# Decoder layer on one Trainium2 core: another distribution of the key and value projections over the batches of a selective scan

## What is computed

```
x = x + mamba(layernorm(x))           # selective scan, 1024 channels, 16 states each
x = x + cross_attention(ctx_1024, keys and values from layernorm(x))   # in the reference's order of arguments (v, k, q)
x = x + ffn(layernorm(x))             # weights binarised, 512 -> 2048 -> 512

# of the scan, per batch element:
xz = rmsnorm(u) @ W_in ;  x, z = split(xz)
x  = silu(conv(x) + b) ;  x_dbl = x @ W_x
dt = softplus(x_dbl[:, :64] @ W_dt + b_dt)
h  = exp(dt * A) * h + (dt * x) * B   # for each of 224 steps
y  = sum over the 16 states of h * C, + x * D
out = u + (y * silu(z)) @ W_out

# of the cross attention, per batch element, 750 context rows:
k = ctx @ Wk + bk ;  v = ctx @ Wv
```

## Time and profile before

| what | us |
|---|---|
| median of three runs | 3401.52 (3398.46 to 3403.88) |
| the profiled execution, its own time | 3404.25 |
| its span in the trace | 3402.7 |
| PE (TensorE matmul) busy | 3155.0 |
| DVE (VectorE) busy | 2577.2 |
| ACT (ScalarE) busy | 2261.3 |
| POOL (GpSimd) busy | 1737.7 |

### The profile page before, as it was taken

The page is one execution under the profiler, slowest core; times in us unless marked ns, Lnnn a source line. Parts: engine busy times, 40 slices in busy tenths (PEclk is TensorE's granted clock), DMA queues, the critical chain, the costliest instruction groups (busy, mean ns, idle before and its releaser), DMA issues. The chain is left out here.

```text
span 3402.7 us, 59176 instructions
## 1 busy us (share of the span) xinstructions
PE 3155.0 (93%) x20736; PEld 2196.4 (65%) x20736; DVE 2577.2 (76%) x4546; ACT 2261.3 (66%) x5049; POOL 1737.7 (51%) x1194
## 2 busy tenths in 40 slices
PE   6699989998999999999998899999999999899999
PEld 5566656665567566666665566666666666578887
DVE  4799999999999999999986577777777777523232
ACT  4678777777777777777764577777777777622222
POOL 2678788788887888778875000100000000055554
PEclk8799999999999999999999899999999999999999
DMA  6677677676767767677665121211211221210100
GB/s 176 178 191 190 180 184 176 174 197 176 185 177 188 187 167 186 184 186 186 171 173 166 54 73 55 89 49 48 85 59 48 73 71 61 63 61 25 48 27 25
DMA packets 286725, 424.98 MB, mean 125 GB/s; under 512 B 28801, under 2 KB 226177, under 8 KB 281954
## 3 DMA queue, kind: packets, MB, share of 16 engines
q1 hardware_dynamic: 278957, 412.62, 44.3%
q10 hardware_dynamic: 7477, 8.59, 0.9%
HBM read 320.12 MB, written 101.02 MB: 124 GB/s over the span
## 5 line engine op out<-in xcount | busy, mean ns | idle before, releaser
L808 POOL TENSOR_TENSOR a_hs<-a_rep,a_bmat 128x896 f32<-128x896 f32 x512 | 1061.1, 2095 | 336.4 <-PE a_yps L319 323.6
L442 ACT ACTIVATE a_states<-a_rep,a_a_neg 128x224 f32<-128x224 f32 x2048 | 795.6, 439 | 194.8 <-DVE a_hs L708 181.9
L701 DVE TENSOR_TENSOR_SCAN a_states<-a_states,a_hs 128x900 f32<-128x900 f32 x384 | 779.0, 2029 | 100.1 <-ACT a_states L442 99.5
L1433 DVE CUSTOM_DVE_ANT_0 b_sc<-sps,early_mask 112x375 f32<-112x375 f32 x1024 | 499.6, 544 | 135.4 <-PE sps L1179 129.5
L1320 ACT ACTIVATE b_sc<-b_sc,b_nmax 112x750 f32<-112x750 f32 x512 | 467.3, 913 | 0.7 <-DVE b_nmax L1439 0.7
L1193 PEld LDWEIGHTS b_tps<-ident,b_sc 112*125 112x125 f32 x3072 | 357.3, 189 | 169.8 <-issue 118.7
L341 PE MATMUL a_work<-early_scan_hT,w_in 128*128 128x224 f32 x2048 | 432.1, 370 | 16.7 <-issue 13.2
L341 PEld LDWEIGHTS a_work<-early_scan_hT,w_in 128*128 128x128 f32 x2048 | 411.7, 202 | 42.0 <-issue 30.2
L1193 PE MATMUL b_tps<-ident,b_sc 112*125 112x112 f32 x3072 | 404.8, 281 | 26.8 <-DVE b_pT L1447 18.2
L708 DVE TENSOR_TENSOR a_hs<-a_states,a_cmat 128x896 f32<-128x896 f32 x384 | 419.0, 1091 | 13.2
L1573 POOL TENSOR_SCALAR b_x_var<-mv 112x2 f32<-112x2 f32 x16 | 3.4, 214 | 814.2 <-DVE mv L1484 814.2
(11 more groups left out here) (193 smaller groups left out, 4735.3 us busy)
## 6 DMA issues: line engine op xcount, KB each, us to landing
a_rep<-du_scratch SPq DMA_DIRECT2D x512, 224.0 KB, 5.5
w_in<-W_in_dram SPq DMA_DIRECT2D x128, 512.0 KB, 4.5
du_scratch<-early_du SPq DMA_DIRECT2D x15, 1792.0 KB, 6.5
ctx<-ctxT_dram SPq DMA_DIRECT2D x48, 500.0 KB, 5.8
v_scratch<-kv_out SPq DMA_DIRECT2D x96, 250.0 KB
k_scratch<-kv_out SPq DMA_DIRECT2D x96, 250.0 KB, 4.3
b_keys<-k_scratch SPq DMA_DIRECT2D x8, 1500.0 KB, 9.2
b_v<-v_scratch SPq DMA_DIRECT2D x8, 1500.0 KB
```

What stands on the lines that cost most here:

```text
L442: e = act.activation(rows(states[:, g % DA, :])[:, q, 1:ROW], rep[tile % REPS][:, j, 0, :], ACT.Exp, scale=a_neg[:, g % SLOTS, q:q + 1])
L701: dve.tensor_tensor_scan(state if g % G4 else whole, state, whole, 0.0, ALU.mult, ALU.add).then_inc(S["scan"], 1)
L808: pool.tensor_tensor(hs[g % RING][:, :, 1:ROW], rep[tile % REPS][:, j, 1, :].unsqueeze(1).broadcast_to([P, Q, L]), bmat[b % 2][:], ALU.mul ...
L1433: dve.tensor_tensor_reduce(out=sc[buffer_of(block)][:, j, cols], in0=sps[0:TT, j, 0:HALF], in1=mask[:, block % 2, cols], scale=-1.0, scala ...
```

## The change

Only the three tuples change, that is, the slots in which units run.

```diff
         first = (16, 17, 22, 24, 25, 28, 29, 31, 33)
-        usual = (1, 3, 5, 12, 13, 18, 20, 21, 24, 25, 29)
-        last_but_one = (1, 2, 3, 4, 5, 12, 13, 17, 18, 19, 20, 21, 22, 23, 24, 25, 26, 28, 29, 30)
-        last = (-1, 1, 2, 3, 5, 6, 7, 12, 13, 14, 15, 16, 17, 18, 19, 20, 21, 22, 23, 24)
+        usual = (1, 3, 5, 6, 12, 13, 18, 20, 21, 24, 25, 29)
+        last_but_one = (1, 3, 5, 6, 12, 13, 18, 20, 21, 22, 24, 25, 28, 29)
+        last = (1, 3, 5, 6, 12, 14, 15, 17, 18, 20, 21, 22, 24)
         kv_slot = ([*first] + [w * SLOTS + BEHIND + at for w in range(1, B - 2) for at in usual]
                    + [(B - 2) * SLOTS + BEHIND + at for at in last_but_one] + [(B - 1) * SLOTS + BEHIND + at for at in last])
```

## The result

| what | before | after |
|---|---|---|
| median of the runs, us | 3401.52 (3398.4 to 3403.9) | 3415.69 (3413.4 to 3426.3) |
| ratio, 95% interval | | 1.0050 (1.0032 to 1.0068) |
| profiled execution, us | 3404.25 | 3420.86 |
| its span | 3402.7 | 3419.3 |
| batches 1 to 13 | 1434.4 | 1473.1 |

The changed kernel is slower, by 14 us in the medians and 16.6 in the profiled executions; 10 were predicted, within 3395 to 3427. The ratio goes by the means of the runs, the times here are medians. All of them are of undisturbed executions; one of the four of run 9 took 5987.64 us and is left out. By the last four rows it is +38.7 - 5.6 - 13.9 - 0.3 = 18.9 us from batch 1 to the end; what lies ahead of batch 1, where nothing changed, was 2.3 us shorter in this execution (batch 1 begins at 197.7 us, not 200.0).

What follows compares the result with a forecast made beforehand. Usual batches were taken as bound by TensorE and VectorE in turn, the last two by their units. +32.9 for the usual batches and -22.9 for the last two gave +10.0 us: 3411.5 us, range 3395 to 3427.

Steps and rivals of the forecast that it cites:

- the room at +16 and +17: TensorE's waits at slots 16 and 17 of a batch's scan: 6.2 + 6.4 = 12.6 us over 13 batches absorb added work.
- the 4.1 us at +8: TensorE's wait before the sum at slot 8: lies ahead of the added unit, so it can't use it.
- The 2.7 at +21: TensorE's wait before the dt products' second half, slot 21: takes up nothing, since lateness returns through ScalarE and the gap moves.
- Rival 1: Usual batches absorb the added unit, with the wait at +21 as room; only the 22.9 gain counts: 3379 us; chance 0.14.
- Usual batches: Batches 1 to 13: 13 added units of 3.5 us each, less 12.6 us of room, cost 32.9 us.
- rival 2: Longer slow clock stretches behind +21 in all 13 usual batches: 13.5 us more, +23.5 in all, 3425 us; chance 0.10.
- DVE's residual wait: VectorE's residual sums wait for the later out projections, about 1 us a batch, adding nothing to the 2.5 per batch.
- The last two batches: Batches 14 and 15 lose 13 units; VectorE's waits fall from 36.9 to 14.0 us, gaining 22.9.
- rival 3: Batches 14 and 15 go down to VectorE's own time: waits shrink to 5, 32 gained, 3402 us; chance 0.11.
- rival 4: Emptied TensorE runs slow in batches 14 and 15, out projections 3 us late in both: +20.5, 3422 us; chance 0.05.

Runs made afterwards that it cites:

- run 9: Kernel before, with a third store buffer in batches 14 and 15 and thirteen of their units shortened to one step of four; 3386.86 us, 0.9955 of before.
- run 1: Changed kernel, with the unit added to batches 1 to 13 at slot 6 (+6) instead of +10; 3405.2 us, 1.0007 of before.
- run 2: Kernel before, with the matmuls of the unit at +9 done twice into the same bank in batches 1 to 13; 3435.93 us, 1.0103 of before.
- run 3: Kernel before, with the matmuls of the unit at +7 done twice into the same bank in batches 1 to 13; 3423.99 us, 1.0063 of before.
- run 4: Kernel before, with thirteen units of batches 14 and 15 doing one of four steps, all copies and stores kept; 3400.84 us, 0.9995 of before.
- run 8: Kernel before, with a third buffer between ScalarE's copies and the stores in batches 14 and 15; 3393.3 us, 0.9972 of before.
- run 7: Changed kernel, with the added unit at +6 instead of +10 and the sum of +20 done twice in batches 1 to 13; 3366.77 us, 0.9893 of before.
- run 10: The kernel of run 7, with half of the matmuls of the unit at +9 done once more; 3354.63 us, 0.9861 of before.
- run 5: Kernel before, with TensorE doing the sum over states of +20 twice in batches 1 to 13; 3378.23 us, 0.9929 of before.

## Why the prediction was right, and where its sizes were off

**The sign and its cause: right.** The forecast was the case in which the added unit finds only the room at +16 and +17. Both went as written: nothing left at +16, 0.15 us at +17 in batch 3, and 10.8 us used, where 12.6 were allowed. That the 4.1 us at +8 can't be used from +10 is shown by run 1, which could use them. That the 2.7 at +21 takes up nothing is shown by its 35.0 us in the change and in runs 1 to 3. Rival 1 is refuted with it.

**Usual batches: +38.7 instead of +32.9.** Divided at the wait of +21, from the sum at +8 to the dt products batches 1 to 13 went from 553.9 to 588.1 us, +34.2; from there to the next +8 from 876.6 to 882.1, +5.5; the ends, ahead of the first +8 and behind the last, make -0.9. The first part is the term itself, 45.5 - 10.8 = 34.7, and stands 1.3 above the forecast. In it, too, the clock is seen: seven batches of the change in which it stays low for longer behind +8 take 45.7 to 46.0 us from +8 to the dt products, the other six 44.4 to 44.7. Before, both kinds took 42.0 to 42.8, because the wait at +16 took up the difference. The second part the forecast had at zero ("behind +21 everything is shifted and nothing changed"). It is rival 2 in part, 5.5 us of its 13.5: of the 13 batches four had a long slow stretch behind +21, and now eight have one. The rival had supposed all 13. That four more got one, and not nine or none, nothing in the prediction foresaw; in this term the forecast stayed near by luck. The Trainium skill, TensorE: Matmul & The Clock Gate, Part 1, says that the gate's steps don't start with the kernel, and batches of equal work that differ by 1.6 us (111.4 and 109.8 before) agree with it.

**DVE's residual wait: right, and costing nothing.** 15.9 us appeared at L723, 1.2 a batch. Run 2 paid as much as the change's usual batches without any such wait.

**The last two batches: -19.5 instead of -22.9, for a reason that was half wrong.** Batch 14 kept 7.8 us of waits instead of 5.4, batch 15 10.6 instead of 8.6. The stores were slow before the next phase's loads began, which the prediction had as the reason: in before, a store of keys landed after 3.6 us in the median of batches 1 to 13, after 6.0 between 1634 and 1800 us, where units stand closer together and none of those loads has been issued, and after 6.8 behind 1800. In the tail of batch 15 the wo issue took 8.30 us and not 5.79: the copy behind it waited 6.85 us, and the one at 1869.60 waited 6.68 for a store. The failed step is the statement that the units bind these batches up to +23 and the stores only behind it. Runs 4, 8 and 9 show what binds instead: relief of PE alone brings 4.3 us, of the stores alone 8.2, of both 15.6. By batch it is 0.6, 5.5 and 5.4 in batch 14, which the stores bound, and 3.7, 2.7 and 10.2 in batch 15, in which PE and stores bound in turn. The change takes away unit, copy and store together and brought 19.5. The size came out nearly right because it was bounded by DVE's waits, which are the same whoever is behind them; for the cause that the prediction named, it was luck.

**The sum.** +38.7 - 19.5 - 0.3 = +18.9 from batch 1 on, -2.3 for batch 0, +16.6 in the profiled executions; +14.2 in the medians. Two terms were off by 5.8 and 3.4 us, both towards slower. Two ends of the prediction's ranges are slips: 13 x (3.5 - 1.09 - 0.7) is 22.2 and not 22.1, and with 2.5 us left in the tail the last two batches would give 27.9, not 29, so that its range begins at 3396. Nothing hangs on either.

Rivals 3 and 4 did not happen: batch 15 stayed 7 us above the 96 of rival 3, and the out projections in batches 14 and 15 were late by 2.4 us in all, not 3 in each.

**Still open.** What makes a slow stretch behind +21 long or short in a given batch; what sets how long the issue of the wo load takes, and whether moving it off ACT would free those 8 us of the tail; what real work could take the place of the filler.

## What to carry to other kernels

An engine's idle time is room only for work that stands ahead of the wait and behind the last thing that another engine needs: 102 us of idle TensorE took up 11 of 45 here, because most of it lay before the added unit or moved along with it. Ask of each wait what it costs behind it as well, since here the clock fell after most waits of 2.2 us and more; if a wait of 2 to 3 us cannot be removed, matmuls that nobody needs may be the cheapest thing to put there. And where two resources bind in turn, as PE and the stores' buffers in the last batch, an experiment that relieves one shows less than half of what both are worth (3.7 and 2.7 of 10.2 us in batch 15).

## What the runs showed of the hardware

- **More matmuls, less time.** Doubling one sum in each of 13 batches (13 x 1.5 = 20 us more work) made the program 26 us faster; filling the wait at +16 too brought 12 more, from run 7 to run 10. Behind a wait of 2.7 us in a 110 us batch dt products and x unit took 2.09 + 4.60 or 2.66 + 5.72 us, where the same work takes 1.78 + 3.19 at the full clock: 1.7 or 3.4 us more. Behind one of 2.2 us at +16 it was 1.06. The Trainium skill, Perfetto Trace Analysis, Matmul Optimizations, asks for matmuls back to back, since the engine scales its power with its use, and these runs agree. The Trainium skill, Perfetto Trace Analysis, Identifying the Most-Contended Engine, says to optimise the most contended engine first, but that TensorE's busy share is no good measure of how close it is to its limit. That agrees too: TensorE was busy for 3155.0 us before and for 3142.3 with 416 more matmuls in run 5.
- **A filled wait moves the fall of the clock.** With +8 filled (run 1), the sum there went from 3.11 to 1.73 us and that at +16 from 1.74 to 2.76. The low clock at +8 had cost before almost nothing, because a wait stood behind it.
- **One DMA issue can hold ScalarE's queue for 12 us.** The load of wo took 5.79 us to issue before, 8.30 after and 12.03 in run 9, where the copy behind it waited 10.2 us, the longest wait of ACT that is left in the last two batches. The six loads ahead of it took 0.3 to 0.4 us each. The shortest issue of wo was 2.32 us, in run 5; what sets the length no run here shows.
